# Turning the scanned rows back ahead of the second norm's turn, in one pass of a graph network

## The chip, the cores and the metric

The kernel runs on one core of a Trainium2 chip. The metric is the device time of one execution in microseconds (us). The engines are named as in the profile: PE is the matrix engine TensorE (PEld its weight loads), DVE is VectorE, ACT is ScalarE, POOL is GpSimd, and SP is the queue that issues plain DMA transfers.

## The reference, cut to what matters

A graph of 100000 nodes with 128 features and 50000 edges, sorted by their target, goes through four layers, each with a residual and a layer norm. What matters here is the first layer, a sum of three sparse passes over the edges, and the second, an MLP over all nodes:

```
Z = X
for _ in range(3):
    Z = segment_sum(w[:, None] * Z[src], dst)         # a sparse pass
x = layernorm(x + concat([X, Z1, Z2, Z3]) @ W0 + b0)
h = relu(concat([x, edge sums, ...]) @ W1 + b1)       # 128 -> 256
x = layernorm(x + x + h @ W2 + b2)                    # 256 -> 128
```

Only nodes that edges touch have a Z that isn't zero. So the kernel computes every node as if it had no edges (a dense stream), and the nodes with edges again later. The sparse passes for the edges run beside the dense stream, because both leave room on the engines.

## The kernel before, in words

Work comes in groups of 512 rows, held in one of four slots `s`; one loop iteration `i` takes the four slots in turn. All rows of a group are four blocks of 128 x 128. The nodes make 49 iterations: 11 alone, 25 beside the first sparse pass (98 groups of edges, plus two empty ones), 13 beside the second pass. This case is about the 25 iterations beside the first pass, 100 steps and the few that empty the pipeline.

Each engine runs its own instruction stream in program order, written by `steps(engine, n, stages...)`: for each step, each stage is issued in the order of the list, for the group that lies `lag` steps back. The engines meet only at counting semaphores (`ready`: this group's input is there; `prior`: the group before has left the buffer, used for PSUM banks, of which each has one; `reuse`: the slot's former group is done). PSUM has eight banks, all in use, one per purpose.

On TensorE a step of this pass is, in order (function, lag): `chain_b1` 1 turns the first norm's rows into bank `bTR`; `chain_a` 0 is the first layer's product (a bias matmul L1000, then L989); `z_turn(0)` 2 turns the gathered, weighted edge rows so that features lie on partitions; `chain_b2` 1 is the first MLP layer (L1034); `chain_d1` 3 turns the second norm's rows into `bTR` (a turn at L938 of `x`), waiting for `ln2_out`; `chain_c` 2 is the second MLP layer (bias L1000, then L1050); `z_back(0)` 3 turns the scanned rows `zT` back into bank `bBK`; `chain_d2` 3 is the last product (L1093). All turns have line L938.

`z_back` has two waits: for `scanned` of its own group (the scan L1856 on VectorE), and for `z_rows` of the group before it, since that frees `bBK`. `z_rows` is ScalarE's copy of `bBK` into `zE` (L1202 with `zE` written). In ScalarE's list it has lag 4, behind `square` 0 and `std` 0 of the step. So the copy of group g - 1 and the turn back of group g belong to the same step.

VectorE's step is: `norm2` 3 (RECIPROCAL L1820, then L1823 `x<-t,ln2rs`, which raises `ln2_out`), `power` 0 with lag 0 (L1808 `ln1vr`), `norm1` 0, `z_weigh` 1 (L1835), `layer2` 2 (L1890, writes `t`, waits for `mlp` of `chain_c`), `power` 1 lag 2 (L1808 `ln2vr`), `z_scan` 2 (L1856), `power` 2 lag 3 (L1808 `ln3vr`), the last norm lag 3.

ScalarE's step is: `square` 0 (L1212 of a bank into `mbuf`), `std` 0 (L1225 `ln1sd`, waits for `ln1vr`), `z_rows` (L1202 `zE`), `x2_out` (L1202 `x2T`), `relu` (L1280), `square` 1 (L1212 of `t`), `std` 1 (L1225 `ln2sd`), `x1_out` (L1202 `x1T`), `square` 2, `std` 2. GpSimd gathers four tiles of edge rows per step once `turned` says that the slot is free; SP issues the loads and stores. At the end of the pass GpSimd waits until all rows of Z1 are stored, and only then gathers for the second pass.

Of the kernel before, what the change touches and what calls it, by code (L numbers as in the profile page):

```python
# [42 lines left out]
def gnn_kernel(nc, x_fm, x_rows, src_g, dst_g, dnext_g, src_flat, dst_flat, w_flat, attr_fm,  # L43
# [5 lines left out]
    EI = -(-EG // SL)  # L49
# [24 lines left out]
    with ctx:  # L74
# [35 lines left out]
        def S(name, s=""):  # L110

            key = f"{first_of(name)[0]}{s if by_slot(name) else ''}"
            if key not in sems:
                sems[key] = ctx.enter_context(nc.semaphore(key))
            return sems[key]
# [158 lines left out]
        def at(eng, name, s, count):  # L274

            count = count + BASE.get(name, 0)
            if isinstance(count, int) and count <= 0:
                return
            eng.wait_ge(S(name, s), count if by_slot(name) else count * SL + (s + 1 - SL))
            if eng.engine == mybir.EngineType.SP:  # L280

                eng.sem_inc(S("go_sp"), 1)

        def ready(eng, name, s, i, n=1):

            at(eng, name, s, (i + 1) * n)
# [5 lines left out]
        def prior(eng, name, s, i):  # L292

            if s > 0:
                at(eng, name, s - 1, i + 1)
            else:
                at(eng, name, SL - 1, i)

        def void(eng, i, s, *counts):

            if not isinstance(i, int) or i * SL + s < EG:
                return False
            for name, done, n in counts:
                if by_slot(name):
                    at(eng, name, s, done * n)
                else:
                    prior(eng, name, s, done)
                eng.sem_inc(S(name, s), n)
            return True
# [40 lines left out]
        def steps(eng, n, *stages, unrolled=False, peeled=0):  # L350

            def iteration(i):
                for s in range(SL):
                    for stage, lag in stages:
                        back = (s - lag) // SL
                        if not isinstance(i, int) or 0 <= i + back < n:
                            stage(i + back, (s - lag) % SL)

            most = max(lag for _, lag in stages)
            apart = 2 if most else 1
            for i in range(apart):
                iteration(i)
            if unrolled:
                for i in range(apart, n - peeled):
                    iteration(i)
            elif n - peeled > apart:
                with eng.Fori(apart, n - peeled) as i:
                    iteration(i)  # L370
            for i in range(max(apart, n - peeled), n + -(-most // SL)):
                iteration(i)

        def all_slots(eng, name, count):

            if by_slot(name):
                for s in range(SL):
                    at(eng, name, s, count)
            else:
                at(eng, name, SL - 1, count)  # L380
# [11 lines left out]
        def seq(k, i):  # L392
            return i + k * EI
# [11 lines left out]
        def moved(k, i, s):  # L405

            return (i + k * (EI if s < EG - (EI - 1) * SL else EI - 1)) * 64
# [457 lines left out]
        def _(pe):  # L865
# [69 lines left out]
            def turn(dst, tiles):  # L935

                for t in range(T):
                    mm = pe.transpose(dst[:, t, :], tiles[t], ident[:, :])  # L938
                return mm

            def z_turn(k):

                def stage(i, s):
                    if void(pe, i, s, ("turned", seq(k if k < 3 else k - 1, i), 1)):
                        return
                    if k == 4:
                        at(pe, "gathered", s, moved(4, i + 1, s))
                        prior(pe, "att_src", s, i)
                    else:
                        ready(pe, "weighted", s, seq(min(k, 3), i))  # L950
                        prior(pe, "scanned", s, seq(min(k, 3), i))
                    turn(bIN, [gat[s][:, t, 0:P] for t in range(T)]).then_inc(S("turned", s), 1)
                return stage
# [8 lines left out]
            def z_back(k):  # L962

                def stage(i, s):
                    if void(pe, i, s, ("back", seq(k, i), 1)):
                        return
                    ready(pe, "scanned", s, seq(k if k < 2 else 3, i))
                    if k < 2:
                        prior(pe, "z_rows", s, seq(k, i))
                    else:  # L970
                        prior(pe, "fin_sum", s, i)
                    turn(bBK, [zT[s][:, t * P:(t + 1) * P] for t in range(T)]).then_inc(S("back", s), 1)
                return stage
# [126 lines left out]
            def node(first):  # L1100
                return ((of("node", chain_b1, first), 1), (of("node", chain_a, first), 0),
                        (of("node", chain_b2, first), 1), (of("node", chain_d1, first), 3),
                        (of("node", chain_c, first), 2), (of("node", chain_d2, first), 3))
# [1 line left out]
            steps(pe, N0, *node(0))  # L1105
            all_slots(pe, "x2T", N0)
            b1, a, b2, d1, c, d2 = node(N0)
            steps(pe, EI, b1, a, (z_turn(0), 2), b2, d1, c, (z_back(0), 3), d2, peeled=1)
            all_slots(pe, "x2T", N0 + EI)
            b1, a, b2, d1, c, d2 = node(N0 + EI)  # L1110
            steps(pe, N2, b1, a, (half(z_turn(1), 0), 2), (half(z_back(1), 0), 3), b2, d1, c, (half(z_turn(1), 1), 2),
# [81 lines left out]
        def _(act):  # L1193
# [22 lines left out]
            def std(kind, k, first=0):  # L1216

                def stage(i, s):
                    c = li(kind, k, i + first)
                    if kind != "node" and void(act, i, s, (f"deviation{k}", c, 1)):  # L1220
                        return
                    vr, sd, _, _ = lns[k]
                    ready(act, f"variance{k}", s, c)
                    last = kind == "node" and k == 2
                    act.activation(sd[s][:, :], vr[s][:, :], ACT.Sqrt, bias=(eps4c if last else epsc)[:, :],  # L1225
                                   scale=(VAR4 if last else 1.0) / P).then_inc(S(f"deviation{k}", s), 1)
                return stage
# [11 lines left out]
            def norm(k, dst, free):  # L1239

                def stage(i, s):
                    if void(act, i, s, (f"ln{k + 1}_out", [x3i, x4i][k - 2]("att", i), 1)):
                        return
                    _, _, rs, nm = lns[k]
                    ready(act, "scale34", s, i)
                    free(i, s)
                    for t in range(T):
                        a = act.activation(dst[s][:, t, :], t2[s][:, t, :], ACT.Identity, bias=nm[s][:, t:t + 1],  # L1248
                                           scale=rs[s][:, t:t + 1])
                    a.then_inc(S(f"ln{k + 1}_out", s), 1)  # L1250
                return stage
# [903 lines left out]
```

## Time and profile before

| | us |
|---|---|
| median of 3 runs | 7268.98 (7268.27 to 7275.58) |
| the profiled execution | 7271.27 |
| its span | 7269.5 |

| engine | busy in the span | share |
|---|---|---|
| PE | 4879.7 | 67% |
| DVE | 4483.0 | 62% |
| POOL | 4686.9 | 64% |
| ACT | 2702.2 | 37% |

The shares are means over stages with different limits. The first sparse pass lies between about 850 and 1780 us of the span. The mean granted TensorE clock over the span is 0.856 of full speed: in the dense stages it is 1.00, in the attention stage (about 4640 to 5730 us) between the two levels, in the last stage 0.50. Timeline rows give the start, the duration, the engine, the line and what was written from what; brackets hold the idle time before and who ended it.

### The profile page before, as it was taken

How to read it: one execution, taken by the hardware profiler on the slowest of the kernel's cores; microseconds unless marked ns; L12 is line 12 of the kernel's file. 1: busy time of each engine (PE TensorE's matmuls, PEld its weight loads, DVE VectorE, ACT ScalarE, POOL GpSimd, SP SyncE). 2: the span in 40 equal slices, each digit the busy share in tenths (PEclk: the TensorE clock that was granted, in tenths of full speed). 3: DMA queues.
4: the chain of work that ended last, by engine and by line, in shares of the span. 5: the costliest groups of instructions: out<-in, count | busy, mean ns of one | idle time of the engine just before them, and what ended most of it. 6: DMA issues, size and time to landing. Idle time of an engine off the chain costs nothing. (4 is left out here: it accounts for less than half of the span.)

```text
span 7269.5 us, 102999 instructions
## 1 busy us (share of the span) xinstructions
PE 4879.7 (67%) x26012; PEld 3292.9 (45%) x26012; DVE 4483.0 (62%) x8275; ACT 2702.2 (37%) x5488; POOL 4686.9 (64%) x4727
## 2 busy tenths in 40 slices
PE   0078799998888899999899999777777411111111
PEld 0055566665666677777544444344444311111110
DVE  8855577776887788888533333688888622222222
ACT  0044455554555344444322222477777400000000
POOL 0067766653775776666466666577777677777777
PEclk9999999999999999999999999888888655555555
DMA  0022366665887898988545555333333222222221
GB/s 21 8 78 83 113 198 196 196 196 165 262 274 231 229 256 251 252 251 252 166 157 162 160 157 161 106 110 105 110 110 106 84 65 66 65 65 65 66 66 55
DMA packets 856086, 1039.14 MB, mean 143 GB/s; under 512 B 141365, under 2 KB 497601, under 8 KB 855844
## 3 DMA queue, kind: packets, MB, share of 16 engines
q1 hardware_dynamic: 705414, 790.38, 35.5%
q0 software_dynamic: 150528, 247.26, 13.0%
q14 instruction: 105, 0.86, 0.0%
q8 instruction: 39, 0.64, 0.0%
HBM read 601.46 MB, written 446.61 MB: 144 GB/s over the span
## 5 line engine op out<-in xcount | busy, mean ns | idle before, releaser
L938 PE MATMUL bank<-ident,gat 128*128 128x128 f32 x2352 | 435.4, 315 | 1347.1 <-DVE zT L1856 1283.3
L1212 ACT ACTIVATE mbuf<-t 128x512 f32<-128x512 f32 x490 | 308.9, 630 | 2066.5 <-DVE t L2094 1323.5
L938 PEld LDWEIGHTS bank<-ident,gat 128*128 128x128 f32 x2352 | 298.4, 162 | 1501.9 <-issue 1158.2
L1835 DVE TENSOR_TENSOR gat<-gat,pays 128x512 f32<-128x512 f32 x392 | 267.4, 682 | 946.2 <-DMA gat<-X,pays 934.3
L1050 PE MATMUL bank<-W2s,hT 128*128 128x128 f32 x6272 | 816.4, 284 | 0.0
L1034 PE MATMUL bank<-x1T,W1x 128*128 128x512 f32 x1568 | 775.4, 607 | 9.1 <-ACT x1T L1202 5.1
L1050 PEld LDWEIGHTS bank<-W2s,hT 128*128 128x128 f32 x6272 | 740.9, 194 | 89.7 <-issue 89.7
L732 POOL DMA_INDIRECT pays<-PAY,s_q x392 | 377.8, 964 | 489.4 <-DVE s_v L1722 340.3
L938 PE MATMUL bank<-ident,x 128*128 128x128 f32 x3136 | 496.7, 282 | 204.8 <-DVE x L1823 187.2
L706 POOL DMA_INDIRECT gat<-X,d_x x392 | 393.0, 1003 | 333.4 <-issue 268.5
L1280 ACT ACTIVATE hT<-bank,b1u 128x512 f32<-128x512 f32 x784 | 496.1, 686 | 245.5 <-PE bank L1037 240.1
L706 POOL DMA_INDIRECT gat<-in_x_rows,pays x392 | 387.3, 988 | 292.7 <-PE bank L938 187.7
L719 POOL DMA_INDIRECT out_rows<-x,d_out x392 | 426.7, 1089 | 224.5 <-ACT x L1248 113.7
L938 PEld LDWEIGHTS bank<-ident,x 128*128 128x128 f32 x3136 | 357.2, 143 | 450.7 <-DVE x L1823 389.4
L706 POOL DMA_INDIRECT gat<-Z2E,pays x392 | 375.7, 958 | 258.8 <-issue 100.1
L706 POOL DMA_INDIRECT gat<-Z1E,pays x392 | 376.4, 960 | 210.6 <-issue 189.6
L1856 DVE TENSOR_TENSOR_SCAN zT<-fB,zT,bank 128x512 f32<-128x512 f32 x392 | 498.2, 1271 | 1.4 <-PE bank L938 1.4
L706 POOL DMA_INDIRECT gat<-X,s_src x392 | 390.0, 995 | 163.6 <-issue 163.3
L706 POOL DMA_INDIRECT x<-in_x_rows,s_src x392 | 417.1, 1064 | 119.5 <-issue 119.2
L739 POOL DMA_INDIRECT VQ<-s_v,s_q x392 | 395.7, 1009 | 119.4 <-issue 112.1
L719 POOL DMA_INDIRECT out_rows<-x,s_out x392 | 393.8, 1005 | 119.3 <-issue 116.6
L1000 PE MATMUL bank<-bias,ones 3*128 3x512 bf16 x784 | 305.3, 389 | 234.8 <-DVE t L2035 130.5
(347 smaller groups left out, 11592.4 us busy)
## 6 DMA issues: line engine op xcount, KB each, us to landing
X<-x SPq DMA_DIRECT2D x686, 256.0 KB, 3.0
fB<-row_s_same SPq DMA_DIRECT2D x392, 256.0 KB, 5.0
xT<-in_x_fm SPq DMA_DIRECT2D x196, 256.0 KB
out_rows<-x SPq DMA_DIRECT2D x196, 256.0 KB
ffB<-rows_last_notlast SPq DMA_DIRECT2D x98, 512.0 KB
Z1T<-zT SPq DMA_DIRECT2D x98, 256.0 KB, 2.1
Z1E<-zE SPq DMA_DIRECT2D x98, 256.0 KB
Z2T<-zT SPq DMA_DIRECT2D x98, 256.0 KB, 5.4
```

The lines of the kernel that those rows point to most:

```text
L706: pool.indirect_dma_start(out=tile[:, t, 0:width], out_offset=None, in_=table, in_offset=bass.IndirectOffsetOnAxis(ap=index[t], axis=0)).t ...
L719: pool.indirect_dma_start(out=table, out_offset=bass.IndirectOffsetOnAxis(ap=index[t], axis=0), in_=rows[t], in_offset=None, bounds_check= ...
L732: pool.indirect_dma_start(out=pays[:, c, :], out_offset=None, in_=PAY, in_offset=bass.IndirectOffsetOnAxis(ap=s_q[:, c:c + 1], axis=0)).th ...
L739: pool.indirect_dma_start(out=VQ, out_offset=bass.IndirectOffsetOnAxis(ap=s_q[:, c:c + 1], axis=0), in_=s_v[:, c:c + 1], in_offset=None, b ...
L938: mm = pe.transpose(dst[:, t, :], tiles[t], ident[:, :])
L1000: pe.matmul(bank_[:, :, :], ones3[:, :], bias3[:, k:k + 1, :].to_broadcast([3, T, P]), start=True, stop=False, skip_group_check=True)
L1034: mm = pe.matmul(bH[h][:, :, :], W1x[:, cols], x1T[s][:, :], start=True, stop=kind != "d")
L1050: mm = pe.matmul(bMLP[:, t, :], hT[h][s][:, t * P:(t + 1) * P], W2s[:, h, :], start=False, stop=h == HC - 1, skip_group_check=True)
L1212: act.activation(sq[k % 3][s % 2], [bT1, t2[s], bSK, t2[s]][k][:, :, :], ACT.Square).then_inc(S(f"squared{k}", s), 1)
L1280: a = act.activation(hT[h][s][:, :], flat(bH[h]), ACT.Relu, bias=b1u[:, h:h + 1])
L1835: dve.tensor_tensor(gat[s][:, :, 0:P], gat[s][:, :, 0:P], pays[:, bass.ds(g, T), 1].bitcast(F32).rearrange("p (t a) -> p t a", a=1).to_bro ...
L1856: dve.tensor_tensor_scan(zT[s][:, :], fB[s][:, :], flat(bIN), zT[s - 1][:, G - 1:G], ALU.mult, ALU.add).then_inc(S("scanned", s), 1)
```

## The change

In TensorE's list for the first sparse pass `z_back(0)` moves from behind the second MLP layer to a place right behind the first MLP layer, ahead of `chain_d1`. Its lag stays 3, its waits stay, no other engine's list is touched, and the second and third pass are as they were.

```
-            steps(pe, EI, b1, a, (z_turn(0), 2), b2, d1, c, (z_back(0), 3), d2, peeled=1)
+            steps(pe, EI, b1, a, (z_turn(0), 2), b2, (z_back(0), 3), d1, c, d2, peeled=1)
```

## Rows read from the trace of the kernel before

**Rows 1.** Windows: duration; busy PE, PEld, DVE, ACT, POOL; clock; DMA share; GB/s

```profile
600.00:800.00 200.00, 167.19 (x978) 115.87 (x977) 109.49 (x213) 99.59 (x214) 152.78 (x156) 1.00 0.29 81
870.00:1770.00 900.00, 830.10 (x5168) 597.83 (x5167) 665.74 (x1148) 492.47 (x1055) 520.10 (x532) 1.00 0.65 195
4700.00:5600.00 900.00, 695.34 (x2556) 405.18 (x2556) 797.59 (x1946) 647.65 (x1243) 646.75 (x622) 0.83 0.38 108
...
804.00:845.00 41.00, 21.87 (x89) 17.16 (x89) 11.14 (x21) 8.81 (x19) 31.26 (x33) 0.59 0.31 90
```

**Rows 2.** Waits, 900 to 1640 us: us in total, times, longest

```profile
PE bank L938 <- DVE x L1823: 48.5, 79, 0.7
```

**Rows 3.** Timeline of PE over one step of the first pass

```profile
1205.54 0.66 PE L938 MATMUL bank<-ident,x 128*128 128x128 f32 x4 [0.62 <-DVE x L1823]
1206.13 0.38 PE L1000 MATMUL bank<-bias,ones 3*128 3x512 bf16 x1
1206.44 2.05 PE L1050 MATMUL bank<-W2s,hT 128*128 128x128 f32 x16
1208.63 0.66 PE L938 MATMUL bank<-ident,zT 128*128 128x128 f32 x4
1209.12 1.06 PE L1093 MATMUL bank<-WsI,x2T 128*128 128x128 f32 x8
...
1212.59 1.88 PE L1034 MATMUL bank<-x1T,W1x 128*128 128x512 f32 x4
1215.19 0.66 PE L938 MATMUL bank<-ident,x 128*128 128x128 f32 x4 [0.72 <-DVE x L1823]
```

**Rows 4.** Timeline of DVE and ACT around the same step

```profile
1201.22 1.27 DVE L1856 TENSOR_TENSOR_SCAN zT<-fB,zT,bank 128x512 f32<-128x512 f32 x1
...
1206.32 0.56 ACT L1202 COPY zE<-bank 128x512 f32<-128x512 f32 x1
...
1208.65 0.69 DVE L1890 SCALAR_TENSOR_TENSOR t<-x,bank 128x512 f32<-128x512 f32 x1 [0.51 <-PE bank L1050]
...
1214.44 0.69 DVE L1823 TENSOR_TENSOR x<-t,ln2rs 128x512 f32<-128x512 f32 x1
...
1215.05 0.68 DVE L1808 TENSOR_REDUCE ln1vr<-mbuf 128x4 f32<-128x512 f32 x1
...
1215.77 0.30 ACT L1225 ACTIVATE ln1sd<-ln1vr,epsc 128x4 f32<-128x4 f32 x1 [2.02 <-DVE ln1vr L1808]
...
1215.97 0.56 ACT L1202 COPY zE<-bank 128x512 f32<-128x512 f32 x1
```

**Rows 5.** Stores of the copied rows, by tile

```profile
L535 SPq DMA_DIRECT2D Z1E<-zE x98: 378/383/398, 874.7 to 1777.1; - x98
```

**Rows 6.** Second pass, timeline: the turn back ahead of the first MLP layer

```profile
1843.52 0.57 ACT L1202 COPY zE<-bank 128x512 f32<-128x512 f32 x1
...
1844.23 0.63 PE L938 MATMUL bank<-ident,zT 128*128 128x128 f32 x4 [1.10 <-ACT zE L1202]
...
1844.70 1.88 PE L1034 MATMUL bank<-x1T,W1x 128*128 128x512 f32 x4
```

**Rows 7.** Timeline of PE at the lower clock, before the pass

```profile
812.49 1.12 PE L938 MATMUL bank<-ident,x 128*128 128x128 f32 x4 [3.98 <-DVE x L1823]
813.53 0.60 PE L1000 MATMUL bank<-bias,ones 3*128 3x512 bf16 x1
814.07 3.78 PE L1050 MATMUL bank<-W2s,hT 128*128 128x128 f32 x16
817.91 1.35 PE L1093 MATMUL bank<-WsI,x2T 128*128 128x128 f32 x8
```

**Rows 8.** Timeline of PE: longest gap of a dense step, and of an attention step

```profile
718.40 0.66 PE L938 MATMUL bank<-ident,x 128*128 128x128 f32 x4 [1.40 <-DVE x L1823]
...
4814.80 1.02 PE L1158 MATMUL bank<-x1T,Wvs 128*128 128x512 f32 x2
4817.95 0.39 PE L1000 MATMUL bank<-bias,ones 3*128 3x512 bf16 x1 [2.13 <-DVE t L2035]
```

## The prediction

> **What bounds the kernel now.** I read the windows first. In the first sparse pass TensorE is busy for 830.1 of 900 us at a clock of 1.00, more than any other engine (DVE 665.7, POOL 520.1) [rows 1]. That looks like a pass bound by TensorE, in which only less work on it would help. The waits say otherwise: TensorE stands still once in every step, 79 times in 740 us for 48.5 us, 0.61 us each, and always in one place, ahead of the turn of the second norm's rows, for VectorE [rows 2]. An engine that waits once per step for a result that itself hangs on that engine is one half of a loop. The reader should follow it in the timeline. TensorE turns the second norm's rows at 1205.54, does the second MLP layer from 1206.13, and VectorE takes that bank at 1208.65 [rows 3, 4]: 3.11 us from the turn. From 1208.65 VectorE and ScalarE need until 1215.13 (1214.44 + 0.69) for the next group's second norm, 6.48 us, and TensorE goes on at 1215.19 [rows 3, 4]. Within those 6.5 us VectorE has the second norm's sum, the scan, the last norm and this norm in program order. 3.11 + 6.48 + 0.06 = 9.65 us is the step. Whatever else TensorE does in the step (last product, first norm's turn, first layer, edge turn, first MLP layer) lies beside VectorE's part of the loop, and ends at 1212.59 + 1.88 = 1214.47, 0.72 us before it is needed [rows 3]. The turn back of the scanned rows at 1208.63 is in that covered part too.
>
> So the idle time is what a reordering could fill, but filling it with covered work gives nothing; only work put on the loop, or taken off, moves the step.
>
> **The change: what it removes.** Behind the second MLP layer the turn back goes, from its start to the next start 1209.12 - 1208.63 = 0.49 us [rows 3]. TensorE's covered part then starts and ends 0.49 us sooner, and nothing hangs on that: ahead of it stands the 0.6 to 0.7 us of idle time. Gain 0; were TensorE's list the bound, it would be at most the whole idle time, 0.6 us per step, and that is the bound below nothing. The last product moves up by 0.49 us; its reader on ScalarE is in the covered part of VectorE's chain behind the scan.
>
> **What it adds: a wait.** At its new place the turn back would come up 0.49 us ahead of the old end of the covered part (the 1214.47 above less 0.49: 1213.98). Its own rows are long there: the scan that wrote them ended at 1201.22 + 1.27 = 1202.49 for the turn at 1208.63 [rows 3, 4], six microseconds ahead. But it also needs the bank `bBK`, and the copy that frees the bank for this group runs on ScalarE in the same step, behind the first norm's deviation, and that waits for the first norm's sum, which on VectorE stands behind the second norm. The rows are the chain: second norm 1214.44 to 1215.13, sum from 1215.05, deviation from 1215.77, copy 1215.97 to 1216.53 [rows 4]. So the bank comes free 1216.53 - 1215.19 = 1.34 us after TensorE now begins the second norm's turn; one step before, 1206.32 + 0.56 - 1205.54 = 1.34 us as well [rows 3, 4]. In the kernel before nobody noticed, because the turn back came up only at 1208.63, 1.75 us after the copy had ended at 1206.88. Its place behind the MLP layer is what hid the copy.
>
> TensorE runs in order, so behind the waiting turn stand the second norm's turn, the second MLP layer and the last product. For the turn ScalarE's copy into `x2T` waits, for the MLP layer VectorE's L1890, and with it the whole loop. POOL and SP have nothing in the moved stage; POOL's gathers and SP's stores only come at a wider distance.
>
> The price of a step, at full clock: the bank comes 1.34 us late; from the end of such a copy to the start of the turn it releases 1844.23 - 1844.09 = 0.14 us pass in the second pass [rows 6]; then 0.49 us of turn back are on the loop [rows 3]. 1.34 + 0.14 + 0.49 = 1.97 us. Nothing gives it back: the copy hangs on the deviation, the sum, the second norm, all of which hang through VectorE's order on the second MLP layer one step before. It is a closed loop, 9.65 us in the step shown (it holds VectorE's jump back), 9.30 us on average over the pass, (1777.1 - 874.7) / 97 [rows 5], and 11.3 to 11.6 us then. Bounds of this term: 0.49 us if the copy were not the last to come, 1.34 + 0.14 + 0.66 = 2.14 us if the turn back costs its whole duration.
>
> One may ask if TensorE would simply let the next turn pass. In the second pass the same stage already stands ahead of other matmuls: the turn back waits 1.10 us for the copy, and the first MLP layer begins only 0.47 us after it [rows 6]. The Trainium skill says the same in "TensorE: Matmul & The Clock Gate", Part 2: only weight loads are pulled ahead, matmuls keep their order. [...]
>
> **How often.** There are 98 edge groups in the pass [rows 5]; the first finds its bank free, so 97 steps pay. 97 x 1.97 = 191 us.
>
> **What the longer gap does to TensorE's clock.** This is the term whose size I can't read. The gap of 0.62 to 0.72 us grows by 0.49 us (work gone from ahead of it) and by 1.48 us (the wait): 1213.98 to 1216.67, 2.7 us in this step and 2.6 us in the usual one. The pass has had nothing like it. The trace has a row on each side. In the dense stage the gap is 1.40 us per step and the clock stays at 1.00; in the attention stage, with a step of about 11.1 us (98 groups from 4640 to 5730 us), a gap of 2.13 us opens in the step shown and the mean clock is 0.83 [rows 1, 8], so a third of that time was spent at 1.2 GHz rather than 2.4. The new step is nearest to the second: the same length, a longer gap, TensorE busy 0.92 x 9.3 = 8.6 of 11.3 us, as 0.77 there (695.3 of 900) [rows 1]. I expect the clock to fall here too. "HAM oscillation — how this bites in real kernels" in the same page of the Trainium skill tells of a kernel that fell to half clock on each turn of its loop because of one wait in it; the attention stage agrees in kind, with its 0.83.
>
> What a fallen clock costs is in the rows just ahead of the pass, where it was down (mean 0.59 in 804 to 845) [rows 1]. From start to start the turn takes 1.04 us there, the bias 0.54, the second MLP layer 3.84 [rows 7], against 0.59, 0.31 and 2.19 at full clock [rows 3]. On the new loop lie turn back, turn, bias and MLP layer: 0.49 + 0.59 + 0.31 + 2.19 = 3.58 us at full clock, 1.04 + 1.04 + 0.54 + 3.84 = 6.46 at half: 2.88 us more per step if the clock is down for all of it in every step, 0 if never. TensorE's other work in the step, 5.35 us at full clock (1209.12 to 1214.47), has 8.0 us of cover now and pays little. With the attention stage's third, 0.34 x 2.88 = 0.98 us. But a clock that falls because of the gap falls just when the loop's matmuls start, so more than an even share meets them; I take 0.4 of it, 1.2 us, and keep 0 and 2.88 for the bounds.
>
> **The sum.** 1.97 + 1.2 = 3.17 us per step, 97 x 3.17 = 307 us. The pass, 850 to 1780 us, gets a third longer. The end of the pass waits for all stores of Z1, and everything behind it (second pass, edges, attention, final pass) is in order behind that, with no slack gathered up: the delay is passed on whole. The profiled execution had 7271.3 us around a span of 7269.5; 7271.3 + 307 = 7578. The median of the runs is 2.3 us lower: 7576, and I say 7575.
>
> **The rivals.** (A, my forecast) The wait on `bBK` closes a longer loop, and TensorE's clock falls in it: 7575. For share and price of the low clock between 0.2 and 0.9 of 2.88 us it is 2.5 to 4.6 us a step, 7515 to 7712. Chance 0.70.
>
> (B) The same wait, but the clock stays at 1.00, or falls so seldom that it can't be seen: 97 x 1.97 = 191, 7460 us. For it: the gap is one piece per step followed by 8.6 us without a break, while in the attention stage the idle time, 205 of 900 us [rows 1], is about as much per step but VectorE's gap of 2.13 us is only a part of it; the dense stage with 1.40 us never shows less than 1.00. Against it: 2.6 us is nearly twice 1.40. Chance 0.22.
>
> (C) The copy isn't what comes last. It decides at the point where ScalarE has copied bank `bBK` before TensorE has finished the first MLP layer, 1213.98 in my step. Then the turn back fills idle time, ends at 1214.47, and the second norm's turn starts at 1215.19 as before: no change, 7269 us; and if the order of the covered part had after all cost something, up to 0.6 us a step come back, 7211 us. For it: TensorE has the idle time exactly there, and the scanned rows are ready. Against it: the copy starts at 1215.97, held by VectorE's second norm, so it would have to come 2.5 us sooner than any row shows, and nothing in ScalarE's or VectorE's list is changed. Chance 0.07 for this, most of it for no change. The last 0.01 is for more than (A) allows.
>
> **How the numbers follow.** What a measurement of this kernel can tell from no change is about 0.2%, 15 us. (A) and (B) are both far slower, 0.93 with the rest; (C) splits into 0.05 within and 0.02 faster. The range is to leave out 0.2: it starts just under (B), 7450, takes in (A) up to 4.3 us a step, 7690, and leaves out (C) and the far end of (A).
>
> **What would show it.** Timeline of the pass: the turn of `zT` starts about 0.14 us after the copy into `zE` ends, with 2.5 us of idle time named for ACT `zE`; the second norm's turn follows it with no wait of its own; steps of 11.3 us where the clock is full. The waits: TensorE for ScalarE's `zE` some 97 times, no longer for VectorE's `x` L1823. Windows: TensorE's busy share of the pass falls from 0.92, and the clock is 1.00 under (B), 0.8 to 0.9 under (A), with L1050 groups of 2.05 us beside some near 3.8. Behind the pass all stages are as long as before. I am wrong if the turn back starts before the copy of its own step, if the steps stay near 9.4 us, or if a stage behind the pass shrinks by what the pass grew.

## The result and the profile after

| | us |
|---|---|
| before, beside the changed kernel | 7272.28 median |
| changed kernel | 7530.23 median (7525.7 to 7531.4, 4 runs) |
| ratio | 1.0354, 95% interval 1.0336 to 1.0372 |
| its profiled execution | 7525.7, span 7523.9 |

The change costs 258 us; the forecast was 7575 us, with a loss of 307. The loss lies in the first sparse pass. The tile's stores show where it ends (count, min/median/max ns, first and last start):

```profile
L535 SPq DMA_DIRECT2D Z1E<-zE x98: 377/383/389, 879.3 to 2034.0; - x98
```

The last of the 98 stores started at 1777.1 before [rows 5] and starts at 2034.0 now, 256.9 us later. The span is 254.4 us longer: all but 2.5 us of it passed on. The second pass takes what it took, 509 us from its first store to its last before and 508 now; its stores in the kernel before, then in the changed one:

```profile
L535 SPq DMA_DIRECT2D Z2E<-zE x98: 382/407/513, 1834.0 to 2342.7; - x98
```

```profile
L535 SPq DMA_DIRECT2D Z2E<-zE x98: 382/407/1040, 2091.1 to 2599.0; - x98
```

The window of the changed kernel's first pass, in the same stretch as before (columns as in rows 1):

```profile
870.00:1770.00 900.00, 714.21 (x4042) 528.53 (x4042) 518.37 (x894) 390.98 (x822) 441.95 (x455) 0.92 0.51 153
```

TensorE is busy for 714 us instead of 830 of 900 [rows 1], and its clock is 0.92 of full speed, not 1.00. Who waited for whom from 900 to 1640 us (us in total, times, longest) in the changed kernel:

```profile
PE bank L938 <- ACT zE L1202: 126.6, 61, 2.2
...
PE bank L938 <- DVE zT L1856: 22.4, 60, 0.6
```

The wait for VectorE's `x` [rows 2] is gone from this list. In its place TensorE waits once in every step for ScalarE's copy into `zE`, 2.08 us each. The second row is a second, shorter wait, of 0.37 us: the turn of the edge rows waits for the scan. It lies in TensorE's covered part, since the copy comes last all the same. Two steps of TensorE in the changed kernel, one with a fallen clock and one without:

```profile
1203.98 1.88 PE L1034 MATMUL bank<-x1T,W1x 128*128 128x512 f32 x4
1207.87 0.66 PE L938 MATMUL bank<-ident,zT 128*128 128x128 f32 x4 [2.02 <-ACT zE L1202]
1208.37 0.60 PE L938 MATMUL bank<-ident,x 128*128 128x128 f32 x4
1208.90 0.38 PE L1000 MATMUL bank<-bias,ones 3*128 3x512 bf16 x1
1209.21 3.33 PE L1050 MATMUL bank<-W2s,hT 128*128 128x128 f32 x16
...
1220.73 0.63 PE L938 MATMUL bank<-ident,zT 128*128 128x128 f32 x4 [2.21 <-ACT zE L1202]
1221.20 0.60 PE L938 MATMUL bank<-ident,x 128*128 128x128 f32 x4
1221.73 0.39 PE L1000 MATMUL bank<-bias,ones 3*128 3x512 bf16 x1
1222.04 2.05 PE L1050 MATMUL bank<-W2s,hT 128*128 128x128 f32 x16
1224.15 1.16 PE L1093 MATMUL bank<-WsI,x2T 128*128 128x128 f32 x8
...
1231.92 0.63 PE L938 MATMUL bank<-ident,zT 128*128 128x128 f32 x4 [2.04 <-ACT zE L1202]
```

And the chain on VectorE and ScalarE that TensorE waits for in the second of them:

```profile
1218.49 0.69 DVE L1823 TENSOR_TENSOR x<-t,ln2rs 128x512 f32<-128x512 f32 x1
1219.10 0.68 DVE L1808 TENSOR_REDUCE ln1vr<-mbuf 128x4 f32<-128x512 f32 x1
1219.82 0.30 ACT L1225 ACTIVATE ln1sd<-ln1vr,epsc 128x4 f32<-128x4 f32 x1 [2.03 <-DVE ln1vr L1808]
1220.02 0.57 ACT L1202 COPY zE<-bank 128x512 f32<-128x512 f32 x1
...
1224.13 0.69 DVE L1890 SCALAR_TENSOR_TENSOR t<-x,bank 128x512 f32<-128x512 f32 x1 [2.38 <-PE bank L1050]
```

The reader should see the whole loop. The second norm's rows are ready at 1219.18, but TensorE stands at the turn back; sum, deviation and copy follow, to 1220.59; 0.14 us later the turn back starts, 0.47 us after it the second norm's turn, which no longer waits, and VectorE gets the MLP's bank at 1224.13. From 1220.73 to 1231.92 the step has 11.19 us, where a short step had 9.30. From 1207.87 to 1220.73 it has 12.86: the second MLP layer took 3.33 us in place of 2.05, and VectorE's jump back of 0.35 us falls into it. Over 85 steady steps of the pass the mean is 12.07 us; before it was 9.39. 97 x 2.68 = 260 us.

### The profile page after: what moved, and what is told of

The parts are those of the page before. It is cut to its first block and busy times, and to the rows that moved or that the text cites. A ratio compares the mean times of both kernels' runs of the same rounds, so it can differ in the third digit from the quotient of the medians.

```text
span 7523.9 us, 102976 instructions
## 1 busy us (share of the span) xinstructions
PE 4964.3 (66%) x26012; PEld 3371.2 (45%) x26012; DVE 4481.1 (60%) x8275; ACT 2710.0 (36%) x5488; POOL 4687.9 (62%) x4727
## 5 line engine op out<-in xcount | busy, mean ns | idle before, releaser
L1050 PE MATMUL bank<-W2s,hT 128*128 128x128 f32 x6272 | 887.6, 300 | 0.0
L1050 PEld LDWEIGHTS bank<-W2s,hT 128*128 128x128 f32 x6272 | 809.0, 209 | 91.8 <-issue 91.8
L1034 PE MATMUL bank<-x1T,W1x 128*128 128x512 f32 x1568 | 773.5, 606 | 9.1 <-ACT x1T L1202 5.5
L1856 DVE TENSOR_TENSOR_SCAN zT<-fB,zT,bank 128x512 f32<-128x512 f32 x392 | 497.9, 1270 | 1.4 <-PE bank L938 1.4
```

Source lines behind the costliest of these rows:

```text
L1034: mm = pe.matmul(bH[h][:, :, :], W1x[:, cols], x1T[s][:, :], start=True, stop=kind != "d")
L1050: mm = pe.matmul(bMLP[:, t, :], hT[h][s][:, t * P:(t + 1) * P], W2s[:, h, :], start=False, stop=h == HC - 1, skip_group_check=True)
L1856: dve.tensor_tensor_scan(zT[s][:, :], fB[s][:, :], flat(bIN), zT[s - 1][:, G - 1:G], ALU.mult, ALU.add).then_inc(S("scanned", s), 1)
```

## The experiments

The theory was that the loss has two parts: a wait for the bank, closed into a loop through VectorE's order (1.89 us a step at full clock), and a clock that falls because of the gap (0.79 us). Rivals: the turn on the loop costs without any wait; the clock alone; the pass is bound by TensorE. Before stands at 7277.25 us median beside the first four, and at 7274.21 beside the last four.

**The wait taken away: `e1_early_copy`** (from the changed kernel, in ScalarE's list)

```
-            steps(act, EI, *node(N0)[:2], (z_rows(0), 4), *node(N0)[2:], peeled=1)
+            steps(act, EI, (z_rows(0), 4), *node(N0), peeled=1)
```

> The changed kernel, with ScalarE's copy of bank bBK (z_rows) moved to the head of ScalarE's step, ahead of square 0 and std 0. Theory (the turn back waits for that copy, which hung on VectorE's first-norm sum): the copy is then done when TensorE has finished the first MLP layer, the 2.0 to 2.2 us of idle time named for zE go, and the step falls from 12.07 to about 9.4 us. A second, smaller loop may then show: scan, edge turn, first MLP layer, turn back, second norm's turn, second MLP layer, t, sum, scan: 9.42 us in place of 9.30. Expected 7272 to 7285 us. Rival 1 (the order itself: the turn back's 0.49 us stands on the loop in any case): 7272 + 97 x 0.49 = 7320. Rival 2 (the bank isn't the wait): 7530.

7275.78 us, ratio 0.9999 (0.9989 to 1.0008): the whole loss is gone, with TensorE's order as changed. Its timeline (TensorE, ScalarE and VectorE):

```profile
1224.04 0.57 ACT L1202 COPY zE<-bank 128x512 f32<-128x512 f32 x1
...
1225.30 0.60 PE L938 MATMUL bank<-ident,zT 128*128 128x128 f32 x4
...
1226.02 0.66 PE L938 MATMUL bank<-ident,x 128*128 128x128 f32 x4
```

The copy ends at 1224.61 and the turn back starts without a wait at 1225.30, in what was idle time. This is rival (C) of the prediction made true, and it gives what (C) gave: no change. The turn as such costs nothing in this kernel. The small second loop that I expected is in the waits (0.4 us for `zT` at L1856) but not in the time: the mean step is 9.39 us, as before.

**The wait alone: `e5_wait_only`** (from the kernel before; nothing is moved)

```
+            def copy_wait(i, s):
+                if isinstance(i, int) and i * SL + s >= EG:
+                    return
+                prior(pe, "z_rows", s, seq(0, i))
-            steps(pe, EI, b1, a, (z_turn(0), 2), b2, d1, c, (z_back(0), 3), d2, peeled=1)
+            steps(pe, EI, b1, a, (z_turn(0), 2), b2, (copy_wait, 3), d1, c, (z_back(0), 3), d2, peeled=1)
```

> The kernel before, with one wait more on TensorE ahead of the second norm's turn: for the same copy of bBK that the changed kernel waits for. The turn back stays behind the second MLP layer. Theory: the wait alone costs 1.34 + 0.14 = 1.48 us a step less what rounding of starts gives back, 97 x 1.44 = 140 us, 7412; TensorE's gap is then 2.1 us, the clock may fall in part of the steps and adds 0 to 60 us: 7405 to 7475. Rival 1 (the loss is the turn on the loop, not the wait): 7272.

7441.21 us, ratio 1.0232 (1.0214 to 1.0249): 164 us, within the range. TensorE in one step, and its clock over the pass:

```profile
1233.14 1.88 PE L1034 MATMUL bank<-x1T,W1x 128*128 128x512 f32 x4
1237.08 0.66 PE L938 MATMUL bank<-ident,x 128*128 128x128 f32 x4 [2.06 <-ACT zE L1208]
1237.66 0.38 PE L1000 MATMUL bank<-bias,ones 3*128 3x512 bf16 x1
```

```profile
870.00:1770.00 900.00, 729.66 (x4371) 535.57 (x4369) 562.83 (x971) 423.58 (x889) 476.59 (x492) 0.96 0.56 166
```

A wait, with no work moved, makes most of the loss, 164 of 258 us. Its short steps have 10.69 us, 1.39 above 9.30; the clock is 0.96.

**The turn back one place further on: `e6_between`** (from the kernel before)

```
-            steps(pe, EI, b1, a, (z_turn(0), 2), b2, d1, c, (z_back(0), 3), d2, peeled=1)
+            steps(pe, EI, b1, a, (z_turn(0), 2), b2, d1, (z_back(0), 3), c, d2, peeled=1)
```

> The kernel before, with the turn back between the second norm's turn and the second MLP layer. Theory: the bank comes free 1.48 us after the second norm's turn starts, that turn takes 0.59 of them, 0.89 us of idle time are left, then 0.47 us of turn back: 1.36 us a step, and two short gaps in place of a long one, so the clock stays at 1.00: 97 x 1.36 = 132, 7404 us (7395 to 7415). Rival 1 (order alone): 97 x 0.49 = 48, 7320. Rival 2 (the clock, not the wait, makes the loss): below 7330.

7450.72 us, ratio 1.024 (1.0223 to 1.0257): 173 us where 132 were expected, and above the range. The wait is near the forecast, the clock isn't. Its TensorE timeline and its window:

```profile
1230.77 0.63 PE L938 MATMUL bank<-ident,gat 128*128 128x128 f32 x4 [0.58 <-DVE zT L1856]
...
1233.83 0.66 PE L938 MATMUL bank<-ident,x 128*128 128x128 f32 x4 [0.72 <-DVE x L1823]
1235.32 0.63 PE L938 MATMUL bank<-ident,zT 128*128 128x128 f32 x4 [0.83 <-ACT zE L1202]
1235.88 0.39 PE L1000 MATMUL bank<-bias,ones 3*128 3x512 bf16 x1
1236.19 3.46 PE L1050 MATMUL bank<-W2s,hT 128*128 128x128 f32 x16
```

```profile
870.00:1770.00 900.00, 751.03 (x4332) 535.41 (x4331) 556.94 (x961) 410.90 (x880) 475.08 (x489) 0.96 0.55 165
```

0.83 us of wait where 0.89 were worked out, and a short step of 10.76 us (10.66 expected). But the clock falls here too: there are two gaps of 0.7 and 0.8 us with one turn between them, and then a second MLP layer of 3.46 us. I had taken two short gaps for harmless, and there is a third, of 0.58 us here, where the turn of the edge rows waits for the scan. The three come to 1.80 us a step between 900 and 1640 us. The mean step is 11.24 us, 0.4 to 0.5 us of it the clock.

**The gap filled: `e3_fill_after`** (from the changed kernel: the first MLP layer's matmuls are done twice)

```
-                for h in range(HC):
+                for h in list(range(HC)) * times:        # times = 2 in this pass
```

> The changed kernel, with the first MLP layer's four matmuls of a group done twice in this pass (same result, 1.88 us more work for TensorE, in the gap ahead of the turn back). Theory (0.79 us of the 2.68 us a step are the fallen clock, because of the gap): the gap shrinks to 0.2 us, the clock is 1.00 throughout, and more work makes the kernel faster: 11.28 us a step, 7272 + 97 x 1.89 = 7455 (7445 to 7470). Rival (the clock is no term of its own): 7530 or more, up to 7530 + 97 x 1.88 = 7712.

7462.29 us, 185 us above the kernel before that ran beside it, where the changed kernel is 258 above its own: some 70 us come back, though TensorE does 1.72 us more in each step. (Eight of these matmuls last 3.60 us, four 1.88.) One of its steps, and the window:

```profile
1230.84 3.60 PE L1034 MATMUL bank<-x1T,W1x 128*128 128x512 f32 x8
1234.74 0.66 PE L938 MATMUL bank<-ident,zT 128*128 128x128 f32 x4 [0.30 <-ACT zE L1203]
...
1236.08 2.05 PE L1050 MATMUL bank<-W2s,hT 128*128 128x128 f32 x16
```

```profile
870.00:1770.00 900.00, 834.15 (x4633) 563.59 (x4633) 555.24 (x959) 417.88 (x878) 471.28 (x486) 1.00 0.55 164
```

The gap is 0.30 us, the clock 1.00, the mean step 11.27 us (11.28 expected). This splits the 2.68 us by measurement: 11.27 - 9.39 = 1.88 us are the wait with the turn, 12.07 - 11.27 = 0.80 us are the clock. The rival, 7530 us or more, is out.

**Covered work doubled: `e4_fill_before`** (from the kernel before: the turn of the edge rows twice)

```
+                    for _ in range(times - 1):            # times = 2 in this pass
+                        turn(bIN, [gat[s][:, t, 0:P] for t in range(T)])
                     turn(bIN, [gat[s][:, t, 0:P] for t in range(T)]).then_inc(S("turned", s), 1)
```

> The kernel before, with the turn of the gathered edge rows done twice in this pass (same result, 0.49 us more work for TensorE in its covered part). Theory (the step is a loop through VectorE, and TensorE's covered part ends 0.6 to 0.7 us early): nothing changes on that loop; the second loop (scan, edge turn twice, first MLP layer, turn, second MLP layer, t, scan) rises to 9.42 us as in the run with the early copy: 7272 to 7285 us. Rival (the pass is bound by TensorE, as its 0.92 busy share suggests): 7272 + 97 x 0.49 = 7320.

7277.12 us, ratio 1.0 (0.9991 to 1.001). The second turn is 0.44 us more work for TensorE in each step (1228.23 - 1227.33 = 0.90 us from the turn's start to the next, 0.46 before), not the 0.49 I had put down. It costs nothing that can be seen and shrinks TensorE's wait, 0.56 to 0.72 us before, to 0.28 us or nothing:

```profile
1220.93 0.66 PE L938 MATMUL bank<-ident,x 128*128 128x128 f32 x4 [0.28 <-DVE x L1825]
...
1227.33 1.06 PE L938 MATMUL bank<-ident,gat 128*128 128x128 f32 x8
1228.23 1.88 PE L1036 MATMUL bank<-x1T,W1x 128*128 128x512 f32 x4
1230.23 0.66 PE L938 MATMUL bank<-ident,x 128*128 128x128 f32 x4
```

So the pass was not bound by TensorE, at a busy share of 0.92, and the loop is VectorE's. If so, shortening VectorE's half must make the kernel faster.

**VectorE's half shortened: `e7_norm_early`** (from the kernel before)

```
-            steps(dve, EI, n2, p0, n1, (z_weigh(0), 1), l2, p1, (z_scan(0), 2), p2, n3, peeled=1)
+            steps(dve, EI, p0, n1, (z_weigh(0), 1), l2, p1, (z_scan(0), 2), (n2[0], 2), p2, n3, peeled=1)
```

> The kernel before, with VectorE's second norm moved from the head of the next step to right behind the scan, so that the last norm's sum and the last norm no longer stand ahead of it. Theory (the loop runs through VectorE's order): that loop falls from 9.30 to about 7.2 us and another becomes the bound: scan, edge turn, first MLP layer, turn, second MLP layer, t, its square and sum, scan: 0.15 + 0.46 + 1.88 + 3.1 + 2.06 + 1.27 = 8.93 us. 9.39 - 8.93 = 0.46 us a step, 7227 us (7215 to 7240). Rival (the loop isn't through VectorE's order, the pass is bound elsewhere): 7272.

7198.53 us, ratio 0.9891 (0.9875 to 0.9908): 1.1% faster, more than I worked out and outside my range. Its timeline around the second norm (VectorE and TensorE):

```profile
1221.01 1.27 DVE L1856 TENSOR_TENSOR_SCAN zT<-fB,zT,bank 128x512 f32<-128x512 f32 x1
...
1222.42 0.69 DVE L1823 TENSOR_TENSOR x<-t,ln2rs 128x512 f32<-128x512 f32 x1
1222.43 0.63 PE L938 MATMUL bank<-ident,gat 128*128 128x128 f32 x4
1222.89 1.88 PE L1034 MATMUL bank<-x1T,W1x 128*128 128x512 f32 x4
...
1224.61 0.60 PE L938 MATMUL bank<-ident,x 128*128 128x128 f32 x4
...
1229.54 1.27 DVE L1856 TENSOR_TENSOR_SCAN zT<-fB,zT,bank 128x512 f32<-128x512 f32 x1
```

The norm is ready at 1223.11, well before its turn at 1224.61. From scan to scan it is 8.53 us, where I had 8.93: in unbroken work the matmuls start 1.72 us after the first MLP layer's start, not 1.88, turn, bias and MLP layer reach VectorE in 2.94 us, not 3.11, and square and sum take 1.99 us, not 2.06. The row of the first MLP layer shows 1.88 us here as well: that duration holds a tail that the next start doesn't wait for.

**Both orders together: `e8_norm_early_both`** (the changed kernel with the edits of `e1_early_copy` and `e7_norm_early`)

> The changed kernel with both: ScalarE's early copy and VectorE's second norm right behind the scan. Theory: no wait for the bank, and the loop through the scan decides. With the turn back ahead of the second norm's turn it holds 0.47 to 0.49 us more than in the kernel with the norm alone: 9.42 us a step, 7275 us (7265 to 7290), some 45 us above that kernel. Rival (once the bank is free in time, the place of the turn back is of no account): the same as that kernel, 7227.

7248.91 us, ratio 0.9961 (0.9947 to 0.9976). The time is below my range, off by the same tails, but the difference that tells the theories apart is near the forecast: 50 us above the norm alone (45 expected), a mean step of 9.16 us against 8.58. One step (TensorE and ScalarE):

```profile
1224.16 1.88 PE L1034 MATMUL bank<-x1T,W1x 128*128 128x512 f32 x4
1225.22 0.56 ACT L1202 COPY zE<-bank 128x512 f32<-128x512 f32 x1
1225.93 0.63 PE L938 MATMUL bank<-ident,zT 128*128 128x128 f32 x4
1226.39 0.60 PE L938 MATMUL bank<-ident,x 128*128 128x128 f32 x4
```

The loop through the scan decides, and the turn back stands in it with 0.46 us (1225.93 to 1226.39), because it comes ahead of the second MLP layer. The changed place is then a cost of its own. The theory's "no wait for the bank" is not quite met: the copy ends at 1225.78, and the turn back starts 1.77 us after the first MLP layer's start, not 1.72. Every fourth step this rest is about 0.3 us, on average 0.12, and 0.46 + 0.12 is the whole 0.58. The part of VectorE and ScalarE from L1890 to the scan takes 1.99 us in both kernels, so the early copy as such adds nothing to it.

**The scan first: `e9_scan_first`** (from the kernel before)

```
-            steps(dve, EI, n2, p0, n1, (z_weigh(0), 1), l2, p1, (z_scan(0), 2), p2, n3, peeled=1)
+            steps(dve, EI, p0, n1, (z_weigh(0), 1), l2, (z_scan(0), 2), p1, (n2[0], 2), p2, n3, peeled=1)
```

> As the kernel with the second norm moved up, and VectorE's scan ahead of the first sum of the second norm, where VectorE waits for ScalarE's square anyway. Theory: the loop through the scan falls to 7.6 us, and what is left is TensorE's own work, 9.30 - 0.6 = 8.7 us, and VectorE's with its short waits for ScalarE, about as much: 8.75 us, 7272 - 97 x 0.64 = 7210 us (7200 to 7230). Rival (VectorE's own order with its waits is longer than that): the same as the norm alone, 7227, or above.

7169.13 us, ratio 0.9852 (0.9836 to 0.9869): the fastest version, 105 us below the kernel before and below the range I gave. Its usual step is 8.34 us, and TensorE has hardly a gap left (window of the pass):

```profile
870.00:1650.00 780.00, 772.93 (x5034) 587.30 (x5033) 642.71 (x1121) 479.08 (x1027) 508.49 (x533) 1.00 0.73 220
```

TensorE is busy for 772.9 of 780 us, and no wait of TensorE is left in the list from 900 to 1640 us: now, for the first time, the pass is bound by TensorE. The rival that VectorE's own order would hold it back is out.

## Why the prediction was right, and where it wasn't

**What bounds the kernel** was read rightly: one wait of 0.6 us per step, on an engine with a busy share of 0.92, was the mark of a loop through VectorE. More covered work cost nothing, and a shorter VectorE half gained 1.1 to 1.5%. The step's mean was given too low, 9.30 for 9.39 us: I had divided the stretch of all stores by their number, and at its end they come closer together, two of them 2.75 us apart.

**The wait on the bank** was right in place and chain, and near in size: 1.97 us worked out, 1.88 measured. The bank came 1.34 + 0.14 us late as read; the turn back puts 0.47 us on the loop, not 0.49, and the second norm's turn behind it takes 0.53 us to the next start in place of 0.59, since it no longer starts from a standstill. In the run with the wait alone, 1.39 us of it are there. This error and that of the clock below, 0.09 and 0.40 us a step, make 48 us, nearly all of the 49 by which the forecast loss was too high.

**The rule that TensorE keeps its order** held: in the changed kernel the second norm's rows are ready at 1219.18, and their turn starts at 1221.20 behind the waiting one.

**The clock** was right in sign and was the one term of the wrong size: 1.2 us forecast, 0.80 measured. I had let all four matmul groups on the loop run at 1.2 GHz for 0.4 of the time, a share that I chose and didn't read; measured are 0.28 of the 2.88 us, near the lower end of (A). The clock also falls later than I argued, not when the loop's matmuls start. In the steps shown turn back, turn and bias run at full speed after the gap, and on the loop only the second MLP layer is slow: 3.33 us, of which 1.28 are the fall. And it falls in about every second step: of the 56 second MLP layers recorded whole between 900 and 1640 us 27 take 3.2 to 3.7 us and 29 take 2.05. Behind a gap of 2.04 us, the most frequent one, 11 are slow and 14 are not. The groups by line over 870 to 1770 us (busy, mean ns of one) say the same for the whole pass; in the kernel before

```profile
L1050 PE MATMUL bank<-W2s,hT 128*128 128x128 f32 x1533 | 196.8, 281 | 0.0
L1034 PE MATMUL bank<-x1T,W1x 128*128 128x512 f32 x384 | 180.8, 593 | 0.9 <-ACT x1T L1202 0.9
```

and in the changed one

```profile
L1050 PE MATMUL bank<-W2s,hT 128*128 128x128 f32 x1200 | 210.8, 348 | 0.0
L1034 PE MATMUL bank<-x1T,W1x 128*128 128x512 f32 x296 | 139.3, 593 | 0.0
```

L1050 went from 281 to 348 ns, L1034 ahead of the gap stayed at 593. The attention stage, with 0.83, was a poor guide: the mean clock of this pass is 0.92. What brings the clock back up within the step isn't shown by a run. "HAM oscillation — how this bites in real kernels" in the Trainium skill's "TensorE: Matmul & The Clock Gate" described the kind of loss, a clock that falls again and again because of a wait in the loop; the filled gap shows it here, with some 70 us back for more work.

**The rivals.** (B), no fall of the clock, was put at 191 us of loss; the kernel with the filled gap, which is (B) made by hand, has 185. (B)'s argument leaned on the dense stage: its gap is not always the 1.40 us of rows 8 but 1.3 to 1.6 us, and its clock stays at 1.00 with all of them. (C), the bank in time, is what the early copy gives.

**What is left open:** why the clock falls in only some of the steps, behind equal gaps too. TensorE's waits summed over a step, and the mean clock, are 1.42 us in one gap and 1.00 in the dense stage; 1.80 in three and 0.96 with the turn back one place on; 2.06, nearly all in one, and 0.96 with the wait alone; 2.43 in two and 0.92 in the changed kernel. No run separates the length of one gap from the sum.

## What to carry to other kernels

Before moving a stage on an in-order engine, look up all its waits, the one for the buffer's release above all, and where in its engine's order the releasing copy stands: a stage placed late may be hiding it. An engine that is 0.92 busy and waits once a step for a result that hangs on itself is not the bound; the gain lies in the other engine's order, here a norm and a scan moved on VectorE, 1.5%. And a gap on TensorE costs more than its length where the clock falls behind it, here 0.80 us a step on top of 1.88.

## What the runs showed of the hardware

The clock fell (mean 0.96 over the pass) in a kernel whose TensorE had three gaps per step, the longest of 0.83 us and 1.80 us in all, while the dense stage with one gap of 1.3 to 1.6 us per step kept 1.00 [rows 1, 8]. It fell in about every second step of the changed kernel, where each step has a gap of 2.0 to 2.2 us. Adding 1.72 us of matmuls in the gap kept it at 1.00 and made that kernel some 70 us faster.

The durations of matmul groups in the profile are not what a group costs the next one. After the first MLP layer the next group starts 1.72 us after its start, with 1.88 shown; after a turn it is 0.47 us with 0.63 shown; after the second MLP layer it is 2.11 us with 2.05 shown (1224.15 - 1222.04 in the changed kernel).
